# An adaptive FFN kernel: 32-bit copies of q1's transposes, an offset taken off through a tenth row of b1, and new orders of all engines

## The chip, the cores and the metric

The kernel runs on one core of a Trainium2 chip. The metric is the device time of one execution in microseconds (us). Engines: PE is TensorE (matrix multiplies and transposes), ACT is ScalarE, DVE is VectorE, POOL is GpSimd, SP is SyncE, whose queue starts the DMA transfers.

## The reference

The input x is 2 x 1024 tokens of 256 numbers. With a condition vector per batch, weights are made for a small down/up pair; then two quantised layers follow, each with its own scale per token and one per weight matrix:

```python
y   = x + relu(x @ w_down) @ w_up                     # w_down 256x64, w_up 64x256, per batch
h   = rmsnorm_quant(y) @ quant(w1).T + b1             # 256 -> 1024
h   = gelu(h)
out = x + rmsnorm_quant(h) @ quant(w2).T + b2         # 1024 -> 256
# act_quant: s = 127 / max|v| per token, round(v*s)/s;  weight_quant: s = 1/mean|w|, clip(round(w*s), -1, 1)/s
```

## The kernel before

Tokens are taken in 8 pairs of tiles (`PAIRS`), a pair being 128 tokens of each of the two batches; s = 0 or 1 (`SLOTS`) is the batch. For a pair k the steps are these.

- `down(n)` (PE, L250) for a group of one or two pairs, `relu(n)` (ACT), `up(k)` (PE, L274), `add_x(k)` (DVE, L735) give y. `square_y(k)` (ACT) sums its squares, `largest_y(k)` (DVE, L653) takes its largest value, `first_steps` and `first_multipliers` make step and multiplier, `quantise_y(k)` (DVE, L704) writes q1.
- q1 is in words of 32 bits whose low half is, as an f16, 1536 + q: adding `MAGIC` rounds and leaves q there. `transpose_q1(k)` (PE, L282) transposes those halves into PSUM, f16; `copy_q1t(k)` (ACT, L534) copies the 512 columns out and takes the 1536 (`OFFSET`) off.
- `first_layer(j, s)` (PE, L301): four matmuls of 512 columns into `h[s]`. `add_bias(j, s)` (PE, L311): b1, split into three bf16 parts by `split_b1(0)` and `split_b1(1)` (DVE, L740), is multiplied by the inverse scale of each token, itself split into three parts by POOL (`inverse_parts`, L1047), so `PARTS` = 9 rows. The inverse scales go through `transpose_inv` (PE) and `copy_invt` (ACT, L540).
- `gelu(j, s)` (ACT, L508) reads `h[s]`; `square_g` (ACT), `largest_g` (DVE, L647), a step and a multiplier, `quantise_first` (slot 0) or `quantise_second` (slot 1) (DVE, L687) write q2, again 1536 + q. `transpose_q2` (PE, L320), `copy_q2t` (ACT, L545, which copies 512 words of 32 bits and leaves the offset in), `second_layer(j, s)` (PE, L336; its first matmul takes the offset off, with the column sums `w2s` made by `sum_w2`), `combine(j, s)` (DVE, L724), and a store by SP once both slots are combined. The last pair is stored slot by slot, slot 0 first. `combine` and `second_layer` of a pair wait for both slots of it or of the pair before.
- Weights: |w1| and |w2| are summed by ACT and DVE (`abs_sum_w1`, `abs_sum_w2`), `weight_sum` (PE) adds over partitions, `total_weights`, `weight_scale`, `inverse_weight_scale` (DVE) give the scale; `round_...`, `lower_...`, `clip_...` make `w1q` and `w2q` in parts (w1: three, w2: two).
- POOL also makes the dequantising factors (`dequantisers(i)`, L996) and adds b2 to x (`add_b2(j)`, L989). `keep_busy` (PE, L233) is matmuls on zeros while PE has nothing to do.

What sets the order is a list of calls written out for each engine (PE from L358, ACT from L560, DVE from L834, POOL from L1066); each engine works through its own list, and semaphores hold it where an input is missing. No engine skips ahead.

Of the kernel before, what the change touches and what calls it, by code (L numbers as in the profile page):

```python
# [4 lines left out]
P = 128  # L5
SLOTS = 2
PAIRS = 8
D, H, F = 256, 64, 1024
DK, FK = D // P, F // P
HALF = 512  # L10
# [9 lines left out]
def adaln_ffn(nc, x_both, down_pack, up_pack, w1_t, w2_t, b1_rows, b2_rows, out):  # L20
# [3 lines left out]
    with ExitStack() as ctx:  # L24
# [38 lines left out]
        w2s = sb("w2s", [P, D], F16)  # L63

# [43 lines left out]
        q1t_view = q1t_ps.rearrange("p (s k t) -> p s k t", s=SLOTS, k=DK)  # L108
        invt_view = t0_flat[:, HALF:HALF + SLOTS * P].bitcast(BF16).rearrange("p (s t) -> p s t", s=SLOTS)
# [42 lines left out]
        w2s_summed, w2s_ready, b1_rest = sem("w2s_summed"), sem("w2s_ready"), sem("b1_rest")  # L152
        up_done, y_ready, xb_ready = sem("up_done"), sem("y_ready"), sem("xb_ready")
# [19 lines left out]
        B1_ROWS = 32 + PARTS  # L173

        def half_rows(n):
            return slice(32 * n, 32 * n + PARTS)
# [55 lines left out]
        def _(pe):  # L232
# [116 lines left out]

            def sum_w2():  # L350
# [16 lines left out]
            keep_busy(6)  # L367
            weight_sum(0)
            down(1)
            transpose_q1(0)  # L370
            keep_busy(3)
            up(1)
            first_layer(0, 0)
            transpose_inv(0)
            first_layer(0, 1)
            add_bias(0, 0)
            down(2)
            transpose_q1(1)
# [12 lines left out]
            sum_w2()
            up(4)
            transpose_inv(2)
            first_layer(2, 0)
            transpose_q2(0, 1)
            add_bias(2, 0)
            first_layer(2, 1)
            transpose_q2(1, 0)
            add_bias(2, 1)
            second_layer(0, 1)  # L400
            transpose_q1(3)
            up(5)
            second_layer(0, 0)
            transpose_q2(1, 1)
# [3 lines left out]
            add_bias(3, 0)  # L408
            second_layer(1, 0)
            second_layer(1, 1)  # L410
            transpose_q2(2, 0)
            down(4)
            add_bias(3, 1)
            transpose_q2(2, 1)
            up(6)
            transpose_q1(4)
            second_layer(2, 0)
            second_layer(2, 1)
            transpose_inv(4)
            first_layer(4, 0)  # L420
            transpose_q2(3, 0)
            add_bias(4, 0)
            first_layer(4, 1)
            up(7)
            transpose_q1(5)
            add_bias(4, 1)
            transpose_q2(3, 1)
            second_layer(3, 0)
# [3 lines left out]
            add_bias(5, 0)  # L432
            second_layer(3, 1)
            transpose_q2(4, 0)
            add_bias(5, 1)
            transpose_q2(4, 1)
            transpose_q1(6)
            second_layer(4, 0)
            transpose_inv(6)
            first_layer(6, 0)  # L440
            second_layer(4, 1)
            add_bias(6, 0)
            transpose_q2(5, 0)
            first_layer(6, 1)
            transpose_q2(5, 1)
            transpose_q1(7)
            add_bias(6, 1)
            second_layer(5, 1)
            transpose_inv(7)
            first_layer(7, 0)  # L450
            add_bias(7, 0)
            first_layer(7, 1)
            add_bias(7, 1)
            second_layer(5, 0)
            transpose_q2(6, 0)
            transpose_q2(6, 1)
            second_layer(6, 0)
            transpose_q2(7, 0)
            second_layer(6, 1)
            transpose_q2(7, 1)  # L460
            second_layer(7, 0)
            second_layer(7, 1)

        @block.scalar
        def _(a):
            a.wait_ge(b1_zero, 1)
            for n in range(2):
                a.dma_start(b1f[half_rows(n), :], b1_rows[:, HALF * n:HALF * (n + 1)]).then_inc(b1_in, 16)
# [95 lines left out]
            round_w1()  # L564
            relu(1)
            lower_w1()
            abs_sum_w2()
            copy_q1t(0)
            copy_invt(0)
            square_y(1)  # L570
            gelu(0, 0)
            relu(2)
            gelu(0, 1)
            copy_q1t(1)
            square_y(2)
            round_w2()
            copy_invt(1)
            lower_w2()
            gelu(1, 0)
            copy_q2t(0, 0)  # L580
            relu(3)
            square_g(0, 1)
            copy_q1t(2)
            gelu(1, 1)
            square_g(0, 0)
            copy_invt(2)
            square_y(3)
            copy_q2t(0, 1)
            gelu(2, 0)
# [3 lines left out]
            copy_q1t(3)  # L593
            square_g(1, 1)
            copy_invt(3)
            square_g(1, 0)
            copy_q2t(1, 1)
            square_g(2, 1)
            gelu(3, 0)
            square_g(2, 0)  # L600
            copy_q2t(2, 0)
            relu(4)
            square_y(5)
            copy_q2t(2, 1)
            gelu(3, 1)
            copy_q1t(4)
            square_g(3, 1)
            copy_invt(4)
            square_g(3, 0)
            copy_q2t(3, 0)  # L610
            gelu(4, 0)
            square_y(6)
# [544 lines left out]
```

## Time and profile before

| | us |
|---|---|
| median of 3 runs (lowest, highest) | 84.02 (83.64, 84.12) |
| the profiled execution, its own time | 84.57 |
| its span, from first to last instruction | 82.9 |
| TensorE clock granted | 1.00 of full speed |

The rows further down come from that one profiled execution. A duration in a timeline is that of one instruction (xN: of N merged); neighbours on an engine overlap somewhat, so the distance between two starts is shorter than the duration. In brackets stands the time that the engine was idle before, and what ended it. The chain of waits is the work that ended last, followed back from the end. "issue" is time in which an engine waited for nothing that the profile shows.

### The profile page before, as it was taken

Reading aid. Unit: us, or ns where it says so; the run is one execution under the profiler, and the core shown is the slowest. Engines: PE = TensorE matmul, PEld = TensorE weight load, DVE = VectorE, ACT = ScalarE, POOL = GpSimd, SP = SyncE. Lnnn points to the kernel's source line nnn. Section 1 sums busy time; section 2 is a strip of 40 time slices with the busy share of each in tenths; the row PEclk is TensorE's granted clock in tenths of the full one; section 3 lists DMA queues with packets and bytes.
Section 4 is the critical chain, followed back from the end, with each engine's and each line's share of the span. In section 5 each row is a group of like instructions: output and inputs, shape, how many; then the busy total and the mean of one; then the engine's idle time right before and its main releaser. Section 6 shows DMA issues by size and latency. Waiting matters only on the chain.

```text
span 82.9 us, 1692 instructions
## 1 busy us (share of the span) xinstructions
PE 68.6 (83%) x507; PEld 39.9 (48%) x507; DVE 71.6 (86%) x153; ACT 65.3 (79%) x127; POOL 44.1 (53%) x113
## 2 busy tenths in 40 slices
PE   4989717599799449899999999999999999948740
PEld 1533215034354134376666594484765662836730
DVE  2158859999899999999999999989999989999950
ACT  0601198838899997969999999999999999999600
POOL 6800007856459989970078183079604872975140
PEclk9999999999999999999999999999999999999999
DMA  0887999999300000000030200300030030002033
GB/s 26 260 296 265 405 342 425 427 415 382 125 4 4 0 12 0 4 0 0 0 126 9 116 11 0 127 0 8 0 127 0 0 127 0 12 21 106 0 127 127
DMA packets 3212, 9.18 MB, mean 111 GB/s; under 512 B 370, under 2 KB 882, under 8 KB 2820
## 3 DMA queue, kind: packets, MB, share of 16 engines
q1 hardware_dynamic: 3168, 9.05, 28.9%
q8 instruction: 4, 0.07, 0.3%
q14 instruction: 4, 0.03, 0.1%
q10 hardware_dynamic: 36, 0.04, 0.1%
HBM read 6.98 MB, written 2.10 MB: 110 GB/s over the span
## 4 chain that ended last, share of the span: by engine, by line
PE 42%; DVE 23%; DMA 10%; issue 8%; POOL 6%; ACT 4%; SPq 3%; DVEq 1%; POOLq 0%; ACTq 0%
PE out_ps L347 11%; DMA w<-w_t 10%; PE h L309 10%; DVE mx L650 7%; PE q2t_ps L333 6%; PE up_ps L279 5%; PE h L316 4%; DVE q L691 4%; DVE w2q L823 2%; POOL rms L1024 2%; PE out_ps L345 2%; PE q2t_ps L290 2%; DVE step L659 2%; DVE y L738 2%; DVE mx L655 2%
## 5 line engine op out<-in xcount | busy, mean ns | idle before, releaser
L650 DVE TENSOR_REDUCE mx<-g 128x1 f32<-128x1024 f32 x16 | 19.4, 1210 | 0.5 <-ACT g L513 0.3
L513 ACT ACTIVATE g<-h,deq 128x1024 f32<-128x1024 f32 x16 | 18.2, 1137 | 0.2 <-PE h L316 0.2
L521 ACT ACTIVATE junk<-g,sq_scale 128x1024 bf16<-128x1024 f32 x15 | 17.5, 1172 | 0.0
L309 PE MATMUL h<-w1q,q1t 128*128 128x512 f16 x64 | 16.0, 380 | 1.5 <-ACT q1t L537 1.5
L347 PE MATMUL out_ps<-w2q,q2t 128*128 128x256 f16 x112 | 14.4, 273 | 0.0
L691 DVE TENSOR_SCALAR q<-g,m 128x1024 f32<-128x1024 f32 (+1 forms) x16 | 13.1, 825 | 0.1
L1009 POOL TENSOR_TENSOR var<-ms,eps_w 128x2 f32<-128x2 f32 (+1 forms) x10 | 2.8, 278 | 19.4 <-ACT junk_y L531 10.1
L347 PEld LDWEIGHTS out_ps<-w2q,q2t 128*128 128x128 f16 x112 | 10.9, 98 | 1.6 <-issue 0.3
L993 POOL TENSOR_TENSOR xx<-xx,b 128x512 f32<-128x512 f32 x8 | 10.1, 1273 | 1.7 <-DMA b<-b_rows 1.6
L548 ACT ACTIVATE q2t<-q2t_ps 128x512 f32<-128x512 f32 x16 | 9.9, 617 | 1.4 <-PE q2t_ps L333 1.4
L333 PE MATMUL q2t_ps<-ident,q 128*128 128x128 f16 x128 | 9.7, 220 | 1.4 <-DVE q L691 1.4
L1011 POOL TENSOR_TENSOR rms<-var,neg_half 128x2 f32<-128x2 f32 (+1 forms) x10 | 9.9, 994 | 0.8
L333 PEld LDWEIGHTS q2t_ps<-ident,q 128*128 128x128 f16 x128 | 7.8, 98 | 4.7 <-DVE q L691 2.9
L309 PEld LDWEIGHTS h<-w1q,q1t 128*128 128x128 f16 x64 | 5.5, 98 | 7.6 <-ACT q1t L537 2.4
L279 PE MATMUL up_ps<-wu,act 128*128 128x512 f32 x16 | 8.6, 619 | 0.1
L531 ACT ACTIVATE junk_y<-y,sq_scale 128x256 bf16<-128x256 f32 x14 | 7.1, 527 | 0.2 <-DVE y L738 0.2
L236 PE MATMUL q2t_ps<-idle 128*128 128x512 bf16 x17 | 5.6, 453 | 1.2 <-DVE idle L834 1.2
L732 DVE SCALAR_TENSOR_TENSOR xx<-out_ps,deq,xx 128x256 f32<-128x256 f32 x14 | 6.3, 473 | 0.2 <-issue 0.2
L738 DVE TENSOR_TENSOR y<-up_ps,xx 128x512 f32<-128x512 f32 x8 | 5.5, 684 | 1.0 <-PE up_ps L279 1.0
L316 PE MATMUL h<-b1f,invt 9*128 9x512 bf16 x32 | 6.2, 393 | 0.0
L655 DVE TENSOR_REDUCE mx<-y 128x2 f32<-128x512 f32 x8 | 5.4, 676 | 0.0
L478 ACT ACTIVATE junk_w<-w 128x1024 bf16<-128x1024 f32 (+1 forms) x3 | 2.7, 910 | 3.2 <-DMA w<-w_t 3.1
(109 smaller groups left out, 113.2 us busy)
## 6 DMA issues: line engine op xcount, KB each, us to landing
xx<-x_both SPq DMA_DIRECT2D x3, 1024.0 KB, 14.0
w<-w_t SPq DMA_DIRECT2D x4, 512.0 KB, 9.3
out<-xx SPq DMA_DIRECT2D x7, 256.0 KB, 2.0
xx<-x_both SPq DMA_DIRECT2D x2, 256.0 KB, 4.9
xx<-x_both SPq DMA_DIRECT2D x1, 512.0 KB, 9.3
upk<-up_pack SPq DMA_DIRECT2D x1, 384.0 KB, 3.5
out<-xx SPq DMA_DIRECT2D x2, 128.0 KB, 1.8
dpk<-down_pack SPq DMA_DIRECT2D x1, 129.0 KB, 2.1
```

The source lines that it names most:

```text
L279: pe.matmul(up_flat, act[:, k, :], wu[:, :, :].rearrange("p s n -> p (s n)"), start=True, stop=True)\
L309: pe.matmul(h[s][:, cols], q1t[:, j % 2, s, c, :], w1q[:, c, cols], start=(c == 0), stop=False)
L316: mm = pe.matmul(h[s][:, HALF * n:HALF * (n + 1)], invt[half_rows(n), j % 2, s, :], upper_half(b1f[half_rows(n), :]), start=False, stop=True)
L333: mm = pe.transpose(q2t_ps[s][:, c, :], low_half(q2[:, j % 2, s, P * c:P * (c + 1)]), ident[:, :])
L347: mm = pe.matmul(out_bank(j, s), q2t[:, j % 2, s, c, :], w2q[:, c, :], start=False, stop=(c == FK - 1))
L513: a.activation(g[:, j % G_RING, s, :], h[s][:, :], ACT.Gelu, scale=deq[:, col:col + 1])\
L521: a.activation(junk[:, j % 2, s, :], g[:, j % G_RING, s, :], ACT.Square, scale=sq_scale[:, 0:1], accum_out=ms[:, col:col + 1]).then_inc(gs ...
L548: a.activation(q2t[:, j % 2, s].rearrange("p k t -> p (k t)").bitcast(F32), q2t_words[s], ACT.Copy)\
L650: v.tensor_reduce(mx[:, col:col + 1], g[:, j % G_RING, s, :], AX.X, ALU.max, apply_absolute_value=True)\
L691: v.tensor_scalar(q2[:, j % 2, s, cols], g[:, j % G_RING, s, cols], m[:, col:col + 1], MAGIC, ALU.mult, ALU.add).then_inc(ready, 1)
L993: p.tensor_tensor(x[:, j], x[:, j], b2[:, :].unsqueeze(1).broadcast_to([P, SLOTS, D]), ALU.add)\
L1011: p.tensor_tensor(rms[:, cols], var[:, cols], neg_half[:, first:last], ALU.pow).then_inc(rms_done, 1)
```

## The change

q1's transposes are copied out of PSUM as 256 words of 32 bits, two f16 halves each, with no offset taken off. The offset comes off through a tenth row: `inv` gets a column that holds -1536 in each half's block, and the matching row of `b1f` gets the column sums of w1q. Those sums are made once by `sum_w1` on PE (a 32-column weight `pick`, whose column 9 is ones, puts them into partition 9 or 41) and added to `b1f` by `add_w1_sums` on DVE. `add_bias(0, s)` and `down(2)`, which uses the same bank, wait for it.

```diff
+        pick = sb("pick", [P, 32], F16)
...
+        q1t_words = q1t_ps.bitcast(F32)
...
-        B1_ROWS = 32 + PARTS
+
+        B1_ROWS = 32 + PARTS + 1
 
         def half_rows(n):
-            return slice(32 * n, 32 * n + PARTS)
+            return slice(32 * n, 32 * n + PARTS + 1)
 
...
                 else:
                     pe.wait_ge(x_in[n], 16)
+                if n == 2:
+                    pe.wait_ge(w1s_ready, 1)
                 if n == 4:
...
                 pe.wait_ge(invt_ready, j + 1)
                 if j == 0:
-                    pe.wait_ge(b1_rest, 2)
+                    pe.wait_ge(w1s_ready, 1)
                 for n in range(F // HALF):
...
+            def sum_w1():
+
+                pe.wait_ge(pick_set, 1)
+                for n in range(F // HALF):
+                    for c in range(DK):
+                        pe.wait_ge(w1_ready[0 if c == 0 else 1 + n], 1)
+                        mm = pe.matmul(q2t_words[1][32 * n:32 * n + 32, :], pick[:, :], w1q[:, c, HALF * n:HALF * (n + 1)],
+                                       start=(c == 0), stop=(c == DK - 1))
+                mm.then_inc(w1_summed, 1)
+
             def sum_w2():
...
             a.wait_ge(b1_zero, 1)
             for n in range(2):
-                a.dma_start(b1f[half_rows(n), :], b1_rows[:, HALF * n:HALF * (n + 1)]).then_inc(b1_in, 16)
+                a.dma_start(b1f[32 * n:32 * n + PARTS, :], b1_rows[:, HALF * n:HALF * (n + 1)]).then_inc(b1_in, 16)
...
                 wait(a, ffn1_done[1], k - 1)
-                a.activation(q1t[:, k % 2].rearrange("p s k t -> p (s k t)"), q1t_ps, ACT.Copy, bias=-OFFSET)\
+                a.activation(q1t[:, k % 2].rearrange("p s k t -> p (s k t)").bitcast(F32), q1t_words, ACT.Copy)\
                     .then_inc(q1t_ready, 1)
...
 
+            def add_w1_sums():
+                v.wait_ge(w1_summed, 1)
+                v.wait_ge(b1_rest, 2)
+                v.tensor_tensor(b1f[0:B1_ROWS, :], q2t_words[1][0:B1_ROWS, :], b1f[0:B1_ROWS, :], ALU.add)\
+                    .then_inc(w1s_ready, 1)
...
             shift_down()
+            split_b1(0)
             scale_up()
             shift_up()
-            split_b1(0)
+            split_b1(1)
             add_x(0)
             largest_y(0)
             first_steps(-2)
...
             p.memset(inv[:], 0.0)
+            p.memset(pick[:], 0.0).then_inc(zero_set, 1)
             p.memset(neg_offset[:], -OFFSET)
+            p.wait_ge(zero_set, 4)
+            for n in range(2):
+                p.memset(inv[:, :, :, 32 * n + PARTS:32 * n + PARTS + 1], -OFFSET)
+            p.memset(pick[:, PARTS:PARTS + 1], 1.0).then_inc(pick_set, 1)
 
             first_scales()
+            weight_constants(0)
             first_weight_scale()
             inverse_parts(0)
-            weight_constants(0)
+            weight_constants(1)
             dequantisers(-1)
...
```

All four lists are rewritten. They are, in the changed kernel, for PE:

```
keep_busy(5) condition_down() condition_up() keep_busy(1) down(0) keep_busy(2) up(0) keep_busy(8) weight_sum(0)
transpose_q1(0) down(1) keep_busy(2) up(1) keep_busy(4) weight_sum(1) transpose_inv(0) sum_w1() first_layer(0,1)
first_layer(0,0) add_bias(0,1) down(2) add_bias(0,0) down(3) transpose_q1(1) up(2) transpose_inv(1) first_layer(1,0)
up(3) add_bias(1,0) first_layer(1,1) transpose_q2(0,0) add_bias(1,1) up(4) transpose_q1(2) sum_w2() first_layer(2,0)
transpose_inv(2) first_layer(2,1) transpose_q2(0,1) add_bias(2,0) up(5) transpose_q2(1,0) add_bias(2,1)
second_layer(0,0) second_layer(0,1) transpose_q1(3) down(4) transpose_inv(3) first_layer(3,0) first_layer(3,1)
add_bias(3,0) transpose_q2(1,1) transpose_q2(2,0) up(6) add_bias(3,1) transpose_q1(4) second_layer(1,0)
second_layer(1,1) transpose_inv(4) first_layer(4,0) first_layer(4,1) add_bias(4,0) add_bias(4,1) transpose_q2(3,0)
second_layer(2,0) transpose_q2(2,1) transpose_q1(5) up(7) transpose_inv(5) first_layer(5,0) first_layer(5,1)
add_bias(5,0) add_bias(5,1) second_layer(2,1) transpose_q2(4,0) transpose_q2(3,1) second_layer(3,0) transpose_q1(6)
second_layer(3,1) transpose_inv(6) first_layer(6,1) transpose_q2(4,1) add_bias(6,1) first_layer(6,0) transpose_q2(5,0)
add_bias(6,0) second_layer(4,1) transpose_q1(7) second_layer(4,0) transpose_inv(7) first_layer(7,1) add_bias(7,1)
first_layer(7,0) transpose_q2(5,1) add_bias(7,0) second_layer(5,0) transpose_q2(6,1) second_layer(5,1)
transpose_q2(6,0) transpose_q2(7,1) second_layer(6,1) second_layer(6,0) transpose_q2(7,0) second_layer(7,1)
second_layer(7,0)
```

ACT:

```
relu(0) abs_sum_w1(0) abs_sum_w1(1) square_y(0) round_w1() lower_w1() relu(1) copy_q1t(0) abs_sum_w2() square_y(1)
copy_invt(0) round_w2() gelu(0,1) relu(2) gelu(0,0) relu(3) copy_q1t(1) lower_w2() copy_invt(1) square_g(0,1)
square_y(2) gelu(1,0) copy_q2t(0,0) gelu(1,1) copy_q1t(2) square_g(0,0) square_y(3) copy_invt(2) square_g(1,0)
gelu(2,0) copy_q2t(0,1) copy_q2t(1,0) gelu(2,1) square_y(4) copy_q1t(3) square_g(2,0) relu(4) copy_invt(3)
square_g(1,1) gelu(3,0) copy_q2t(2,0) copy_q2t(1,1) square_y(5) copy_q1t(4) gelu(3,1) square_g(2,1) copy_invt(4)
square_g(3,1) gelu(4,0) copy_q2t(3,0) gelu(4,1) copy_q1t(5) square_g(3,0) copy_q2t(2,1) copy_invt(5) square_y(6)
gelu(5,0) gelu(5,1) copy_q2t(4,0) copy_q2t(3,1) square_g(4,0) copy_q1t(6) square_y(7) copy_invt(6) square_g(4,1)
copy_q2t(4,1) gelu(6,1) copy_q2t(5,0) gelu(6,0) copy_q1t(7) square_g(5,0) copy_invt(7) square_g(5,1) gelu(7,1)
copy_q2t(5,1) gelu(7,0) square_g(6,0) copy_q2t(6,1) quantise_last() copy_q2t(6,0) square_g(6,1) copy_q2t(7,1)
square_g(7,0) copy_q2t(7,0)
```

DVE, after six memsets:

```
set_cond() scale_down() shift_down() split_b1(0) scale_up() shift_up() split_b1(1) add_x(0) largest_y(0)
first_steps(-2) first_multipliers(-2) abs_sum_w1() quantise_y(0) total_weights(0) weight_scale(0)
inverse_weight_scale(0) round_w1(0) lower_w1(0) round_w1(2) clip_w1(0) abs_sum_w2() lower_w1(2) clip_w1(1) clip_w1(2)
total_weights(1) add_x(1) weight_scale(1) largest_y(1) inverse_weight_scale(1) add_w1_sums() first_steps(-1)
round_w2() first_multipliers(-1) lower_w2() quantise_y(1) clip_w2(0) largest_g(0,1) largest_g(0,0) add_x(2)
second_step(0) largest_y(2) first_steps(0) first_multipliers(0) quantise_first(0) add_x(3) clip_w2(1) quantise_y(2)
second_multiplier(0) largest_y(3) quantise_second(0) largest_g(1,0) add_x(4) first_steps(1) first_multipliers(1)
largest_y(4) quantise_first(1) copy_w2_sums() largest_g(1,1) add_x(5) quantise_y(3) largest_g(2,0) combine(0,0)
combine(0,1) first_steps(2) second_step(1) largest_y(5) second_multiplier(1) first_multipliers(2) quantise_second(1)
quantise_first(2) largest_g(2,1) quantise_y(4) largest_g(3,0) first_steps(3) first_multipliers(3) second_step(2)
quantise_y(5) second_multiplier(2) add_x(6) combine(1,1) combine(1,0) quantise_first(3) quantise_second(2)
largest_y(6) largest_g(3,1) largest_g(4,0) largest_g(4,1) first_steps(4) second_step(3) first_multipliers(4) add_x(7)
quantise_first(4) second_step(4) second_multiplier(3) quantise_y(6) quantise_second(3) second_multiplier(4)
combine(2,1) combine(2,0) largest_y(7) quantise_second(4) largest_g(5,0) largest_g(5,1) first_steps(5) combine(3,1)
first_multipliers(5) second_step(5) quantise_first(5) second_multiplier(5) combine(3,0) quantise_second(5)
quantise_y(7) largest_g(6,1) largest_g(6,0) combine(4,0) second_step(6) combine(4,1) second_multiplier(6)
first_steps(6) first_multipliers(6) quantise_second(6) quantise_first(6) largest_g(7,1) second_step(7) largest_g(7,0)
second_multiplier(7) combine(5,0) quantise_last() combine(5,1) first_steps(7) scale_last() first_multipliers(7)
quantise_first(7) square_last() combine(6,0) combine(6,1) combine(7,1) combine(7,0)
```

POOL, after its memsets:

```
first_scales() weight_constants(0) first_weight_scale() inverse_parts(0) weight_constants(1) dequantisers(-1)
inverse_scale(1) inverse_parts(1) add_b2(0) dequantisers(0) inverse_scale(2) inverse_parts(2) add_b2(1)
dequantisers(1) add_b2(2) inverse_scale(3) inverse_parts(3) dequantisers(2) inverse_scale(4) inverse_parts(4)
add_b2(3) dequantisers(3) inverse_scale(5) inverse_parts(5) add_b2(4) dequantisers(4) inverse_scale(6)
inverse_parts(6) add_b2(5) dequantisers(5) inverse_scale(7) inverse_parts(7) dequantisers(6) add_b2(6) add_b2(7)
dequantisers(7) dequantisers(8)
```

## Rows read from the trace of the kernel before

**Rows 1.** The page, part 1: busy time by engine.

```profile
PE 68.6 (83%) x507; PEld 39.9 (48%) x507; DVE 71.6 (86%) x153; ACT 65.3 (79%) x127; POOL 44.1 (53%) x113
```

**Rows 2.** Busy time in stretches of core 0; columns: stretch, its length, then each engine.

```profile
12.00:16.00 4.00, 2.85 (x19) 1.51 (x19) 3.85 (x12) 3.63 (x11) 2.77 (x7) 1.00 1.03 418
...
28.00:32.00 4.00, 2.24 (x14) 1.24 (x14) 4.00 (x8) 3.81 (x7) 3.63 (x8) 1.00 0.02 6
...
36.00:44.00 8.00, 8.00 (x65) 5.42 (x65) 7.78 (x17) 7.95 (x16) 3.11 (x10) 1.00 0.10 35
```

**Rows 3.** The chain of waits in order of time: start us, us, what.

```profile
23.71 1.74 issue
...
27.85 1.62 DVE w2q L823
...
35.40 0.62 PE q2t_ps L333 x8
...
40.12 1.73 PE h L309 x8
```

**Rows 4.** Timeline of DVE: start us, us, engine, line, operation [idle before].

```profile
16.61 0.76 DVE L745 SCALAR_TENSOR_TENSOR b1f<-b1f,later 41x512 f32<-41x512 bf16 x1
...
23.68 1.85 DVE L691 TENSOR_SCALAR q<-g,m 128x1024 f32<-128x1024 f32 x1
...
26.64 1.21 DVE L650 TENSOR_REDUCE mx<-g 128x1 f32<-128x1024 f32 x1
27.77 1.69 DVE L823 TENSOR_SCALAR w2q<-w 128x1024 f16<-128x1024 f32 x1
...
30.84 0.74 DVE L691 TENSOR_SCALAR q<-g,m 128x1024 f32<-128x1024 f32 x1
31.50 0.68 DVE L655 TENSOR_REDUCE mx<-y 128x2 f32<-128x512 f32 x1
32.10 1.21 DVE L650 TENSOR_REDUCE mx<-g 128x1 f32<-128x1024 f32 x1
```

**Rows 5.** Timeline of POOL.

```profile
17.42 0.26 POOL L985 TENSOR_SCALAR eps_w<-iws 128x2 f32<-128x2 f32 x1
...
23.71 1.28 POOL L993 TENSOR_TENSOR xx<-xx,b 128x512 f32<-128x512 f32 x1 [1.62 <-DMA b<-b_rows]
...
27.65 1.27 POOL L993 TENSOR_TENSOR xx<-xx,b 128x512 f32<-128x512 f32 x1
```

**Rows 6.** Timeline of ACT.

```profile
17.83 0.38 ACT L543 ACTIVATE invt<-q2t_ps 128x256 bf16<-128x256 bf16 x1 [1.53 <-PE q2t_ps L298]
...
19.10 1.10 ACT L513 ACTIVATE g<-h,deq 128x1024 f32<-128x1024 f32 x1
...
53.96 0.64 ACT L537 ACTIVATE q1t<-q2t_ps 128x512 f16<-128x512 f16 x1
54.44 1.17 ACT L513 ACTIVATE g<-h,deq 128x1024 f32<-128x1024 f32 x1
55.43 0.66 ACT L548 ACTIVATE q2t<-q2t_ps 128x512 f32<-128x512 f32 x1
55.91 0.46 ACT L543 ACTIVATE invt<-q2t_ps 128x256 bf16<-128x256 bf16 x1
56.17 1.23 ACT L521 ACTIVATE junk<-g,sq_scale 128x1024 bf16<-128x1024 f32 x1
...
57.31 1.22 ACT L521 ACTIVATE junk<-g,sq_scale 128x1024 bf16<-128x1024 f32 x1
...
69.48 2.20 ACT L513 ACTIVATE g<-h,deq 128x1024 f32<-128x1024 f32 x2
```

**Rows 7.** Timeline of PE, the second `down`.

```profile
12.92 0.66 PE L263 MATMUL h<-xx,wd 128*64 128x128 f32 x8 [0.42 <-DMA xx<-x_both]
```

**Rows 8.** Timelines of DVE and of SP's queue, the end.

```profile
79.72 0.88 DVE L732 SCALAR_TENSOR_TENSOR xx<-h,deq,xx 128x256 f32<-128x256 f32 x2 [0.71 <-POOL deq L1016]
...
80.23 0.81 SPq L225 DMA_DIRECT2D out<-xx  x2
```

More of the change, by code:

```diff
@@ L408, in _ @@
             add_bias(3, 0)
+            transpose_q2(1, 1)
+            transpose_q2(2, 0)
+            up(6)
+            add_bias(3, 1)
+            transpose_q1(4)
             second_layer(1, 0)
             second_layer(1, 1)
[L411 to L418, printed above, removed]
             transpose_inv(4)
             first_layer(4, 0)
+            first_layer(4, 1)
+            add_bias(4, 0)
+            add_bias(4, 1)
             transpose_q2(3, 0)
-            add_bias(4, 0)
-            first_layer(4, 1)
+            second_layer(2, 0)
+            transpose_q2(2, 1)
+            transpose_q1(5)
             up(7)
[L425 to L428, printed above, removed]
             transpose_inv(5)
@@ L564, in _ @@
             round_w1()
+            lower_w1()
             relu(1)
-            lower_w1()
+            copy_q1t(0)
             abs_sum_w2()
-            copy_q1t(0)
+            square_y(1)
             copy_invt(0)
-            square_y(1)
+            round_w2()
+            gelu(0, 1)
+            relu(2)
             gelu(0, 0)
-            relu(2)
-            gelu(0, 1)
+            relu(3)
             copy_q1t(1)
+            lower_w2()
+            copy_invt(1)
+            square_g(0, 1)
             square_y(2)
-            round_w2()
-            copy_invt(1)
-            lower_w2()
             gelu(1, 0)
             copy_q2t(0, 0)
-            relu(3)
-            square_g(0, 1)
+            gelu(1, 1)
             copy_q1t(2)
-            gelu(1, 1)
             square_g(0, 0)
+            square_y(3)
             copy_invt(2)
-            square_y(3)
+            square_g(1, 0)
+            gelu(2, 0)
             copy_q2t(0, 1)
-            gelu(2, 0)
             copy_q2t(1, 0)
@@ L858, in _ @@
             round_w1(2)
+            clip_w1(0)
+            abs_sum_w2()
+            lower_w1(2)
             clip_w1(1)
-            lower_w1(2)
-            clip_w1(0)
             clip_w1(2)
+            total_weights(1)
             add_x(1)
-            split_b1(1)
+            weight_scale(1)
             largest_y(1)
+            inverse_weight_scale(1)
+            add_w1_sums()
             first_steps(-1)
+            round_w2()
             first_multipliers(-1)
+            lower_w2()
@@ L868, in _ @@
             quantise_y(1)
-            abs_sum_w2()
+            clip_w2(0)
+            largest_g(0, 1)
             largest_g(0, 0)
             add_x(2)
-            total_weights(1)
+            second_step(0)
             largest_y(2)
             first_steps(0)
-            weight_scale(1)
             first_multipliers(0)
-            inverse_weight_scale(1)
             quantise_first(0)
+            add_x(3)
+            clip_w2(1)
             quantise_y(2)
-            round_w2()
-            largest_g(0, 1)
@@ L882, in _ @@
-            lower_w2()
-            second_step(0)
-            clip_w2(0)
-            clip_w2(1)
             second_multiplier(0)
-            add_x(3)
+            largest_y(3)
             quantise_second(0)
-            largest_y(3)
             largest_g(1, 0)
+            add_x(4)
             first_steps(1)
+            first_multipliers(1)
+            largest_y(4)
+            quantise_first(1)
             copy_w2_sums()
-            first_multipliers(1)
-            quantise_first(1)
@@ L895, in _ @@
-            add_x(4)
+            largest_g(1, 1)
+            add_x(5)
             quantise_y(3)
-            largest_g(1, 1)
+            largest_g(2, 0)
+            combine(0, 0)
+            combine(0, 1)
+            first_steps(2)
             second_step(1)
+            largest_y(5)
             second_multiplier(1)
-            largest_y(4)
+            first_multipliers(2)
             quantise_second(1)
-            largest_g(2, 0)
-            first_steps(2)
-            combine(0, 0)
@@ L905, in _ @@
-            first_multipliers(2)
-            combine(0, 1)
+            quantise_first(2)
             largest_g(2, 1)
-            quantise_first(2)
-            second_step(2)
-            add_x(5)
-            second_multiplier(2)
             quantise_y(4)
-            quantise_second(2)
-            combine(1, 0)
-            combine(1, 1)
-            largest_y(5)
             largest_g(3, 0)
@@ L1106, in _ @@
             inverse_parts(4)
+            add_b2(3)
             dequantisers(3)
@@ L1116, in _ @@
             inverse_parts(7)
-            add_b2(5)
             dequantisers(6)
```

217 lines of the change are left out of this document (113 added, 104 removed).

## The prediction

> **What bounds the kernel now.** The first view is the page's table of busy time [rows 1]: VectorE (DVE) 71.6 us, TensorE (PE) 68.6, ScalarE (ACT) 65.3 of a span of 82.9. Three engines so close say that no engine alone is "the" bound, so the second view is busy time by stretch [rows 2]. From 36 to 44 us PE is busy 8.00 of 8.00, ACT 7.95, DVE 7.78: all full. From 28 to 32 us DVE is full (4.00) and PE is busy only 2.24. So the head is DVE's, the middle is everybody's. The chain of waits [rows 3] agrees: it runs on DVE up to 35.40, then on PE. What the reader should see in its head are two pieces: an "issue" of 1.74 at 23.71 and a 1.62 us `w2q` at 27.85.
>
> The timelines of DVE and POOL explain them [rows 4, 5]. The same form of `quantise` takes 0.74 us at 30.84 but 1.85 at 23.68, just as POOL's b2 addition of 1.28 starts at 23.71. The lowering of w2, L823, takes 1.69 at 27.77, beside the next b2 addition (27.65, 1.27 long). If both are worth the 0.74 of the undisturbed one, 1.85 - 0.74 = 1.1 and 1.69 - 0.74 = 0.95 were lost: **2.05 us of DVE stall in the stage that DVE sets**, both on the chain. The reduction at 26.64 (1.21 long, 1.13 to the next start) shows no such stretch, nor does the one at 32.10 beside POOL's later additions. The Trainium skill says why: GPSIMD Engine Reference, Specifications, has the two engines share SBUF interfaces, with contention for DVE operations in a two-port mode or with two SBUF inputs. The trace agrees by the 1.85 against 0.74.
>
> **The change, part by part.** I work with slots, the distance from one start to the next, since neighbours overlap. On ACT [rows 6]: q1t copy 54.44 - 53.96 = 0.48, gelu 0.99, q2t copy 0.48, invt copy 0.26, square 57.31 - 56.17 = 1.14. On DVE [rows 4]: quantise 0.66 (31.50 - 30.84), `largest_y` 0.60, `largest_g` 1.13. On PE [rows 3]: eight first-layer matmuls 1.73, so 0.87 for one `first_layer`.
>
> *Copy as words.* 512 f16 become 256 words. The invt copy also moves 256 elements out of PSUM and has a slot of 0.26 [rows 6]; the q2t copy shows that 512 words cost 0.48, as 512 halves do, so price goes by elements. I take 0.27: 8 x 0.21 = **1.7 us off ACT**, 0.6 of it in the head. Bounds: nothing (if it stayed at 0.48) and 1.8.
>
> *`sum_w1`.* Four 512-column matmuls before `first_layer(0, 1)`: 4 x 0.216 = 0.87 on PE, once. Its nearest row is that of the same form with 128-column weights; I keep from nothing to the whole 1.73 of eight as the bounds. The Trainium skill, TensorEngine Tiling, Key Properties, lets different tiles run in parallel; here only the second and third matmul are neighbours on different tiles, and by that the sum would be 0.65.
>
> *`add_w1_sums`, `split_b1(1)`.* The addition on DVE reads PSUM once and is 512 columns: like an `add_x` or `largest_y`, 0.60. `split_b1(1)`, 0.76 at 16.61 [rows 4], with slot 0.68, moves to before `add_x(0)`, where DVE waits for `up(0)` and later for w1. DVE's sum stays even. `split_b1(0)` ahead of `scale_up` makes `up(0)` some 0.3 later; that is hidden while DVE and ACT wait for w1's DMA, and costs its 0.3 if w1 came sooner.
>
> *w2's weights earlier.* DVE's `abs_sum_w2` (a 1024-column reduction: 1.13) comes at about 15.3, before the last parts of w1, in place of after `quantise_y(1)`. Is w2 there? x of pair 1 landed at 12.92 [rows 7]; at 418 GB/s [rows 2] the 1.0 MB of w2 behind it needs 2.5 us more: 15.4. Just in time. But it pushes `clip_w1` and `add_x(1)` back by 1.2 us: `add_x(1)` began 0.6 before the split at 16.61, at 16.0, and now begins at 17.3.
>
> *POOL.* `weight_constants(0)` now stands before the first inverse parts: two operations, the first 0.26 with 0.33 to the next start [rows 5], some 0.5 together (the memsets of `pick` and of the new `inv` columns fall into POOL's wait for the first squares and cost nothing; if that wait were gone, they would cost some 0.3), so `transpose_inv(0)` slips from 17.5 (its copy began at 17.83 [rows 6]) to 17.9. Behind it on PE wait `sum_w1` (to 18.9) and both first layers (to 20.6). `add_w1_sums` gets its sums at 19.0 and is done at 19.6; the bias follows the layers, at 20.95. So **the first gelu starts at 21.05 instead of 19.10** [rows 6]: 1.95 us late. That hurts less than it sounds: ACT fills the wait with `square_y(1)` and with `round_w2`, which used to come behind both gelus, and part of the 1.53 that it waited before the first invt copy [rows 6] goes.
>
> *b2 additions.* `add_b2(0)` still waits for its DMA, to 23.7, but DVE then runs `largest_g(0, 0)` and `add_x(2)`, which don't stall; `round_w2` and `lower_w2` have run by 21.3, and `add_b2(1)` comes only at 30.8. By the new order the 2.05 us of stall are gone, but for up to 0.65 at `first_steps(1)`.
>
> **The sum, by walking the new order with these slots** (each operation starts when its engine is free and its inputs are done; 0.1 us per hand-over). At some places I compare with the time at which the kernel before had done the same set of operations:
> - DVE starts `largest_g(1, 0)` at 29.65; before 32.10 [rows 4]. 2.4 ahead, 2.05 of it from the stall; `add_w1_sums` (0.6) is made up by the moved split (0.68).
> - PE starts the first layers of pair 3 at 38.16; before 40.12 [rows 3]. It has done `down(4)` by then (eight matmuls, 1.0), which it had not, and lacks one `transpose_q2` (0.45): 2.0 + 1.0 - 0.45 = 2.5 ahead.
> - From there on PE is the tight engine. Counted in the same way at pairs 5 and 6, its lead grows by 0.3 only, because nothing on PE became cheaper.
> - The last gelu ends at 68.2; before 69.48 + 2.20, so 71.6 [rows 6]: 3.4 ahead. Slot 1 of the last pairs goes first, so that `largest_g(7, 1)` and ACT's last copies no longer stand in one line behind the last gelu.
> - The last combine ends at 76.1 by the walk. For the work of DVE after 36.6 the walk sets 2.2 us less than the trace before holds for the same set (small steps and stalls); half of it or less fits into gaps that the walk has. So 77.0; before 80.60 [rows 8]. 3.6 ahead.
> - The stores of slots 0 and 1: SP waits for slot 0 first, and slot 0 is now combined last, so both issues (0.81 together [rows 8]) come behind the last combine, where before one did: **0.4 worse**.
>
> 3.6 - 0.4 = 3.2 us off the span. The profiled execution took 84.57 (span 82.9, 1.67 around it), 0.55 over the median of 84.02. 82.9 - 3.2 = 79.7 of span, 81.4 for that execution, and 84.02 - 3.2 = **80.8 us** for the median. About 0.5% (0.4 us) is what a measurement can tell from no change.
>
> **Rivals.**
> - *Only the head's lead stays.* The last pairs give nothing, since DVE has its line of work behind the last gelu (80.60 - 71.68 = 8.9 us before) either way. 2.4 - 0.4 = 2.0: 82.0. For it: DVE was full to the end. Against: slot 1 first takes a reduction out of the last line. Chance 0.20.
> - *The stalls come back elsewhere.* All eight b2 additions (1.27 each) are still made. If a quantise or step starts at the start of two of them, 2.05 is lost again, and ACT's 1.7 less 0.4 remains: -1.3, 82.7. By the rule of the GPSIMD Engine Reference cited above nothing is avoided for good, only placed; by it a shift of half a microsecond decides. Chance 0.15, half of what a blind placement would deserve, since long reductions stand at most places.
> - *Copy by words costs as before* (0.48): 3.2 - 1.7 = 1.5 off, 82.5. The invt row speaks against it. Chance 0.03.
> - *Slower: the late start is never made up.* Place: POOL's inverse parts, `sum_w1` and `add_w1_sums` in line before the first gelu, on an ACT that has little idle time afterwards. +1.95 + 0.4 - 1.7 = +0.65: 84.7. It decides if ACT has no work to fill the wait, that is if the first gelu starts past 21.5 or w2 lands past 16.5, with all of DVE's list (in order) behind `abs_sum_w2`. Against: DVE's own sum is what set the head. Chance 0.10.
> - *A lead lost half-way* through new waits in a rewritten order of three full engines, to within 0.4 us of before: 0.07.
>
> The forecast (79.7 to 81.6; its low end is the walk without DVE's 0.9) keeps 0.45.
>
> **How the numbers follow.** Faster by over 0.5% are the forecast, the first three rivals: 0.45 + 0.20 + 0.15 + 0.03 = 0.83. Same 0.07, slower 0.10. Low end 79.5, a little under the walk's own 79.9. The high end takes in the rivals at 82.0, 82.5 and 82.7 with `sum_w1` at its dear end (+0.9): 83.5. What lies outside is the slower case and most of the even one.
>
> **What the profile would show.** q1t copies of about 0.39 us each; first gelu at 21 on slot 1; no quantise or `w2q` over 1 us before 30 us; PE full from about 33; last gelu ending near 68 to 69; both stores issued behind the last combine, near 77. Wrong if DVE stands waiting for gelus between 22 and 36, if `abs_sum_w2` waits for its DMA, or if the last gelu ends past 70.5.

## The result, and the profile after

The changed kernel takes 81.14 us (median of 4 runs, 81.11 to 81.39); the kernel before took 84.07 in the same series. The ratio is 0.965, with a 95% interval of 0.958 to 0.972. In a later series it was 81.36 against 83.56, ratio 0.972 (0.966 to 0.978). The forecast was 80.8 in a range from 79.5 to 83.5. Medians and ranges from here on leave out the slow runs, those over 1.5% above the fastest of their kernel.

| | before | after |
|---|---|---|
| the profiled execution, its own time, us | 84.57 | 81.12 |
| its span | 82.9 | 79.4 |
| first w1 sum on DVE starts | 11.31 | 10.65 |
| first gelu starts | 19.10 | 20.27 |
| last gelu ends | 71.68 | 68.00 |
| last two combines start | 79.72 | 75.84 |

The lines behind this table that stand nowhere else, first of the kernel before, then of the changed kernel (w1 sum, last gelu, last combines):

```profile
11.31 0.69 DVE L795 TENSOR_REDUCE asum<-w 128x1 f32<-128x512 f32 x1 [0.94 <-DMA w<-w_t]
```

```profile
10.65 0.69 DVE L819 TENSOR_REDUCE asum<-w 128x1 f32<-128x512 f32 x1 [0.15 <-DMA w<-w_t]
...
66.87 1.13 ACT L531 ACTIVATE g<-h,deq 128x1024 f32<-128x1024 f32 x1
...
75.84 0.88 DVE L750 SCALAR_TENSOR_TENSOR xx<-h,deq,xx 128x256 f32<-128x256 f32 x2 [0.32 <-issue]
```

One difference isn't the kernel's. The weights landed 0.66 us earlier in the profile after. The start of the first w1 sum moves by over two microseconds between the profiles of this study (10.65 to 13.00), so from here on I compare profiles by the distance **from the start of the first gelu to the start of the last pair of combines**: 60.62 before, 55.57 after (and 55.56 in a second profile of the same kernel). The kernel before has one profile only, and that execution took 84.57 us, where its medians are 83.42 to 84.07; so a difference to its profile may be too large. The first gelu itself comes 7.79 us behind the first w1 sum before and 9.62 after. Together 68.41 against 65.19: 3.2 us of kernel, of which the store order gives 0.4 back (below).

The page of the changed kernel, parts 1 and 2, answers to [rows 1]:

```profile
PE 69.2 (87%) x515; PEld 40.8 (51%) x516; DVE 69.6 (88%) x154; ACT 63.6 (80%) x127; POOL 44.9 (57%) x117
...
PE   3997937759999999999999999996999999949910
```

DVE is busy 2.0 us less, though it got an addition; ACT 1.7 less; PE 0.6 more. Busy time by stretch answers to [rows 2]:

```profile
20.00:24.00 4.00, 4.00 (x30) 1.86 (x29) 3.57 (x7) 3.73 (x6) 3.47 (x10) 1.00 0.18 69
...
28.00:32.00 4.00, 4.00 (x29) 2.40 (x29) 3.96 (x9) 4.00 (x11) 3.02 (x10) 1.00 0.01 2
...
52.00:60.00 8.00, 7.36 (x71) 5.21 (x71) 8.00 (x19) 8.00 (x20) 5.07 (x11) 1.00 0.10 35
```

PE, which had 2.24 of 4 between 28 and 32 us, is now full from 20 us on (to 52); the prediction had expected it full from about 33. DVE's timeline answers to [rows 4]:

```profile
18.11 0.68 DVE L769 TENSOR_TENSOR b1f<-q2t_ps,b1f 42x512 f32<-42x512 f32 x1
...
19.56 0.70 DVE L847 TENSOR_SCALAR w2q<-w 128x1024 f16<-128x1024 f32 x1
...
25.79 0.75 DVE L709 TENSOR_SCALAR q<-g,m 128x1024 f32<-128x1024 f32 x1
...
29.24 1.21 DVE L668 TENSOR_REDUCE mx<-g 128x1 f32<-128x1024 f32 x1
...
30.96 0.51 DVE L677 SCALAR_TENSOR_TENSOR step<-mx,over_q 128x3 f32<-128x3 f32 x1
...
43.19 1.67 DVE L727 TENSOR_SCALAR q<-y,m 128x256 f32<-128x256 f32 x2
...
67.80 0.82 DVE L677 SCALAR_TENSOR_TENSOR step<-mx,over_q 128x1 f32<-128x1 f32 x1
```

The two long operations of the head are gone: w2q 0.70 for 1.69, quantise 0.75 for 1.85. But two others are long that weren't: the pair of `quantise_y(5)` at 43.19 (1.67, where its like takes 0.61) and a step at 67.80 (0.82, where its like takes 0.15). POOL's timeline has a b2 addition at each, and one at the smaller stretch at 30.96 (0.51):

```profile
30.17 1.28 POOL L1018 TENSOR_TENSOR xx<-xx,b 128x512 f32<-128x512 f32 x1
...
43.38 1.33 POOL L1018 TENSOR_TENSOR xx<-xx,b 128x512 f32<-128x512 f32 x1
...
67.33 2.51 POOL L1018 TENSOR_TENSOR xx<-xx,b 128x512 f32<-128x512 f32 x2
```

ACT's copies and the first gelu, to be read beside [rows 6]:

```profile
22.95 0.38 ACT L555 ACTIVATE q1t<-q2t_ps 128x256 f32<-128x256 f32 x1
23.24 1.14 ACT L524 ACTIVATE w2q<-w,neg_round 128x1024 f16<-128x1024 f32 x1
...
20.27 1.11 ACT L531 ACTIVATE g<-h,deq 128x1024 f32<-128x1024 f32 x1 [0.51 <-PE h L322]
```

### The profile page after: what moved, and what is told of

The parts are those of the page before. It is cut to its first block, busy times and chain, and to the rows that moved or that the text cites. A ratio compares the mean times of both kernels' runs of the same rounds, so it can differ in the third digit from the quotient of the medians.

```text
span 79.4 us, 1717 instructions
## 1 busy us (share of the span) xinstructions
PE 69.2 (87%) x515; PEld 40.8 (51%) x516; DVE 69.6 (88%) x154; ACT 63.6 (80%) x127; POOL 44.9 (57%) x117
## 4 chain that ended last, share of the span: by engine, by line
PE 42%; DVE 18%; issue 10%; DMA 9%; POOL 9%; ACT 3%; SPq 3%; DVEq 2%; POOLq 0%; ACTq 0%
PE h L315 11%; DMA w<-w_t 9%; PE out_ps L353 9%; DVE mx L668 6%; PE up_ps L285 5%; PE h L322 4%; PE q2t_ps L339 4%; DVE q L709 4%; DVE q L727 3%; DVE xx L750 3%; POOL rms L1036 3%; POOL rms L1049 2%; PE out_ps L351 2%; DVE mx L673 1%; PE out_ps L269 1%
## 5 line engine op out<-in xcount | busy, mean ns | idle before, releaser
L1036 POOL TENSOR_TENSOR rms<-var,neg_half 128x2 f32<-128x2 f32 (+1 forms) x10 | 11.5, 1146 | 0.8
L709 DVE TENSOR_SCALAR q<-g,m 128x1024 f32<-128x1024 f32 (+1 forms) x16 | 11.4, 730 | 0.1
L566 ACT ACTIVATE q2t<-q2t_ps 128x512 f32<-128x512 f32 x16 | 9.4, 604 | 0.0
L240 PE MATMUL q2t_ps<-idle 128*128 128x512 bf16 x21 | 6.6, 440 | 1.3 <-DVE idle L858 1.2
L727 DVE TENSOR_SCALAR q<-y,m 128x256 f32<-128x256 f32 x16 | 6.1, 425 | 0.0
L322 PE MATMUL h<-b1f,invt 10*128 10x512 bf16 x32 | 6.0, 392 | 0.0
```

What stands on the lines that cost most here:

```text
L322: mm = pe.matmul(h[s][:, HALF * n:HALF * (n + 1)], invt[half_rows(n), j % 2, s, :], upper_half(b1f[half_rows(n), :]), start=False, stop=True)
L566: a.activation(q2t[:, j % 2, s].rearrange("p k t -> p (k t)").bitcast(F32), q2t_words[s], ACT.Copy)\
L709: v.tensor_scalar(q2[:, j % 2, s, cols], g[:, j % G_RING, s, cols], m[:, col:col + 1], MAGIC, ALU.mult, ALU.add).then_inc(ready, 1)
L1036: p.tensor_tensor(rms[:, cols], var[:, cols], neg_half[:, first:last], ALU.pow).then_inc(rms_done, 1)
```

## The experiments

"The distance" below is that from first gelu to last combines. Where a profile's start was late (last section), its span isn't used.

**The cheaper copy.** In the changed kernel:

```diff
-  a.activation(q1t[...].bitcast(F32), q1t_words, ACT.Copy)
+  a.activation(q1t[...], q1t_ps, ACT.Copy)
```

> The changed kernel with q1t copied as 512 halves (no offset taken off, so the result stays), as dear as before. Theory (ACT's list is one of the tight ones, its 8 x 0.21 us count): +1.7 us if ACT sets the pace throughout, 82.8; between +0.8 and +1.7 is on its side. Rival (PE and DVE set the pace, ACT's saving falls into its own waits): at most +0.3, 81.4.

Measured: 82.31 us (82.21 to 82.36), ratio to the kernel before 0.987 (0.984 to 0.990), where the changed kernel has 0.965 and 0.972. The copies are 0.59 to 0.77 us long, for 0.37 to 0.43; the distance is 56.55, 0.98 more than after. ACT's and DVE's timelines of this kernel:

```profile
23.14 0.60 ACT L555 ACTIVATE q1t<-q2t_ps 128x512 f16<-128x512 f16 x1
```

```profile
43.70 0.61 DVE L727 TENSOR_SCALAR q<-y,m 128x256 f32<-128x256 f32 x2
```

So of 8 x 0.21 = 1.7 us about 1.0 shows. That is the low side of what the theory allowed, and clearly more than the rival's 0.3. It is a net value: with its operations some 0.3 us later, this kernel has `quantise_y(5)` at 43.70 undisturbed (0.61 for 1.67), a stall of 1.06 less, and only 0.4 more of stall elsewhere. The dear copies by themselves may thus cost more than 1.0; how much isn't shown.

**The two halves of the orders.** The old and the new list of each engine have points where both have done the same set of calls. Cut there, and one order is put ahead and the other behind.

```diff
 # newhead_oldrest: new lists up to the cut, old lists behind it; oldhead_newrest: the reverse
 # cut: PE behind 28 calls, ACT 28, DVE 50, POOL 13 (keep_busy, sum_w1, add_w1_sums not counted)
```

> The changed kernel, its four lists cut where both orders have done the same set of calls (PE behind 28 calls, ACT 28, DVE 50, POOL 13): new order ahead of the cut, old order behind it. Theory (the head's lead of 2.4 us, mostly DVE stalls that are gone, is the larger part): 84.07 - 2.4 = 81.7, a little less if the cheaper copies still count behind the cut. Rival (the rest's order made the gain): 83.4 or more.

> The same cut the other way: old order ahead of it (with sum_w1 and add_w1_sums put in), new order behind. Theory: the stalls of 2.05 us in DVE's head stay, only the copies and the last pairs help, 83.0 to 83.5. Rival (the rest's order made the gain): 81.5.

And both old, so that only the copies and the sums are new:

> Old orders on all engines, with the copies as words, sum_w1 behind first_layer(0, 1) and add_w1_sums behind quantise_y(1). Theory (stalls of the head stay; the copies give some of their 1.7 us, sum_w1 and add_w1_sums take 0.6 to 1.2 of it in the head): 83.3 to 84.1. Rival (the copy alone is the change, orders are neutral): 81.5.

The rows come from three series, in which the kernel before took 83.42 (old, old), 83.53 (the two mixed ones) and 83.56 (new, new); the ratios compare best. In the last column the first number moves with the start of the execution as well: among all profiles with the new head it is 8.99 to 10.71.

| orders (all with word copies) | time, us | ratio to before, interval | w1 sum to first gelu + distance |
|---|---|---|---|
| old, old | 84.25 | 1.009 (1.005 to 1.014) | 9.16 + 59.13 = 68.29 |
| old head, new rest | 83.80 | 1.005 (1.001 to 1.010) | 9.16 + 58.23 = 67.39 |
| new head, old rest | 82.86 | 0.992 (0.989 to 0.996) | 9.62 + 57.45 = 67.07 |
| new, new | 81.36 | 0.972 (0.966 to 0.978) | 9.62 + 55.57 = 65.19 |

Three things follow. The copies and sums without new orders are no gain. By the runs they lose 0.8 us (84.25 against 83.42); by the profiles they come out even (68.29 against 68.41; the executions profiled took 85.17 and 84.57, both over their medians). The first gelu waits for the sums (9.16 in place of 7.79), and the distance gives back 1.5 (59.13 for 60.62). DVE's timeline says where from:

```profile
25.79 0.78 DVE L707 TENSOR_SCALAR q<-g,m 128x1024 f32<-128x1024 f32 x1
...
28.80 1.44 DVE L845 TENSOR_SCALAR w2q<-w 128x1024 f16<-128x1024 f32 x1
```

With the gelu late, the first quantise misses the b2 addition, which ended at 24.31 (0.78 for 1.85), and w2q meets it later (1.44 for 1.69). That is 1.3 of the 1.5. Behind the head this kernel has 0.6 more of such stalls than before, so with the old orders the cheaper copies themselves gave between 0.2 and 0.8. It also means that the stall of 2.05 which the last two expectations took to stay was 0.75 (0.78 and 1.45 in the kernel with the old head and the new rest).

The head alone brings 68.29 - 67.07 = 1.2 us, not the 2.4 of its lead; the rest alone brings 0.9. Both bring 3.1, one microsecond more than the two apart. By the ratios it is 1.4, 0.3 and 3.1. Against the expectations, on the scale of 84.07: the new head with the old rest comes to 83.4, the rival's number and not the theory's 81.7, though the rival's reason (the rest alone made the gain) is refuted by the third kernel, which comes to 84.5 where 83.0 to 83.5 was expected. Old with old comes to 84.8, outside its 83.3 to 84.1. So neither half carries the gain alone. What in the new order of the rest gives its part wasn't separated, apart from the last pairs and the stores below.

With the old rest behind the new head, the b2 additions collide at once, as DVE's timeline of that kernel shows beside POOL's (POOL first):

```profile
30.20 4.19 POOL L1017 TENSOR_TENSOR xx<-xx,b 128x512 f32<-128x512 f32 x3
```

```profile
30.58 0.91 DVE L676 SCALAR_TENSOR_TENSOR step<-mx,over_q 128x3 f32<-128x3 f32 x1
31.94 1.31 DVE L708 TENSOR_SCALAR q<-g,m 128x1024 f32<-128x1024 f32 x1
33.77 1.02 DVE L726 TENSOR_SCALAR q<-y,m 128x256 f32<-128x256 f32 x2
```

Undisturbed these three take 0.15, 0.74 and 0.61, so 1.7 us of stall stand within four microseconds of the cut; the changed kernel has 0.6 at the same three (0.51, 0.74 and 0.83).

**Is the stall POOL's, and is it on the path?** In the kernel before:

```diff
 # before_b2_late
-            add_b2(0) ... add_b2(1) ... add_b2(2)  add_b2(3)   (each at its old place)
             inverse_parts(3)
+            add_b2(0)
+            add_b2(1)
+            add_b2(2)
+            add_b2(3)
```

> The kernel before, with the first four b2 additions of POOL moved behind inverse_parts(3), nothing else changed. Theory (the two additions at 23.7 and 27.6 stall quantise and w2q by 2.05 us on the path): the two DVE operations fall from 1.85 and 1.69 to about 0.75, and the time by 1 to 2 us, to 82.0 to 83.0, less what the additions collide with in their new place. Rival (the long operations are slow for another reason, or the stall is not on the path): both stay long, or they get short and the time stays at 84.0.

```profile
23.80 0.78 DVE L691 TENSOR_SCALAR q<-g,m 128x1024 f32<-128x1024 f32 x1
...
26.82 0.68 DVE L823 TENSOR_SCALAR w2q<-w 128x1024 f16<-128x1024 f32 x1
...
37.93 0.62 DVE L659 SCALAR_TENSOR_TENSOR step<-mx,over_q 128x3 f32<-128x3 f32 x1
...
41.46 1.23 DVE L659 SCALAR_TENSOR_TENSOR step<-mx,over_q 128x1 f32<-128x1 f32 x1
```

The cause of the two long operations is shown: quantise falls from 1.85 to 0.78 and w2q from 1.69 to 0.68 when nothing but POOL's list is changed, and the additions, now from 37.26 to 42.67, stretch the steps there. The distance falls by 1.42 (60.62 to 59.20). The time falls less: 83.16 against 83.42, ratio 0.997 (0.993 to 1.001), which doesn't stand out from no change, where 1 to 2 us were expected. By the time alone, the rival's second form (they get short and the time stays) isn't excluded. I leave open why. The times of the kernel before spread from 83.06 to 84.24 us in one series, and its profile is one of 84.57. An addition that begins when b2's transfer lands, 0.03 us behind the start of a quantise, may well hit it in some executions and miss it in others; that wasn't tried.

Then both kernels without the additions:

> The kernel before without the eight additions of b2 (left out: + b2 in the output). Theory (they stall DVE by 2.05 us in the head and by about 1 us later, all in a full DVE list): 84.07 - 2.5 = 81.5, within 0.7. Rival (stalls are absorbed): 83.6 or more.

> The changed kernel without the eight additions of b2 (left out: + b2 in the output). Theory (the new place of the additions already avoids most stalls): 81.14 less 0.3 to 1.0, so 80.1 to 80.8, clearly less than what the kernel before gains. Rival (the stalls came back elsewhere): as much as before, 2 us or more.

The kernel before gains 1.36 us (82.06 against 83.42, ratio 0.981, 0.974 to 0.988), which the rival (83.6 or more) doesn't allow; its distance falls by 2.06. DVE now waits for gelus:

```profile
L650 DVE TENSOR_REDUCE mx<-g 128x1 f32<-128x1024 f32 x16 | 19.4, 1213 | 1.9 <-ACT g L513 1.8
```

DVE waited 0.5 us there in the kernel before. So a part of the stall was worth nothing: ACT would not have been ready. The changed kernel gains 0.49 in distance (55.08), in line with the theory's 0.3 to 1.0, while its time (81.58, 81.02 to 82.11, from four runs) can't be told from no change; in its profile the first `add_x` began 2 us later than after, most of it because PE's first matmuls took about twice as long (last section).

**The last pairs.** New order up to the end, old order behind it:

```diff
 # old_tail, DVE (PE and ACT in the same way)
-            largest_g(7, 1)
-            second_step(7)
             largest_g(7, 0)
...
+            largest_g(7, 1)
+            second_step(7)
```

> The changed kernel with the old order behind a common cut near the end (PE behind 92 calls, ACT 76, DVE 121, POOL 35): slot 0 of the last pair is reduced first, though its gelu still comes second. Theory (slot 1 first takes one reduction out of the line behind the last gelu): +0.7 to +1.3 us, with the reduction of slot 1 behind that of slot 0. Rival (DVE is full to the end either way, order is neutral): within 0.3.

```profile
69.44 1.22 DVE L667 TENSOR_REDUCE mx<-g 128x1 f32<-128x1024 f32 x1 [1.49 <-ACT g L530]
...
72.69 1.21 DVE L667 TENSOR_REDUCE mx<-g 128x1 f32<-128x1024 f32 x1
```

From the last gelu's start to the last combines it takes 9.74 us, against 8.97 after: +0.77. The first part of the way is nearly unchanged (46.72 against 46.60). DVE idles 1.49 where it had the other slot's reduction to do. The old order of the last combines gives 0.4 of it back (next experiment). The time is 81.58 us (two runs, 81.55 and 81.60) against 81.36, ratio 0.975 (0.965 to 0.985): +0.2 where +0.7 to +1.3 was expected, and not clear of no change.

This experiment overstates the swap, because it is an order that no kernel had: in the kernel before, slot 0's gelu comes first as well, and DVE doesn't idle at that reduction. From the end of the last gelu to the start of the last combines the two orders as they are take 8.04 before (71.68 to 79.72) and 7.84 after (68.00 to 75.84), and 8.38 in the kernel with the new head and the old rest. So the swap of slots is worth 0.2 to 0.5 us, stalls included, and the stores below take 0.4 back.

**The store order.**

```diff
-            for s in range(SLOTS):
+            for s in (1, 0):
                 sp.wait_ge(out_ready[s], PAIRS)
```

> The changed kernel with SP waiting for slot 1 before slot 0 at the last pair. Theory (two stores behind the last combine cost one issue): one issue of about 0.4 us leaves the end, 80.7 us against 81.14. Rival (the second store's issue and flight are hidden by the first's): 81.1, no difference.

> SP waits for slot 1 before slot 0 at the last pair, in one series with the changed kernel. Theory (one store issue less behind the last combine): 0.4 us below it, and in the profile 3.2 us from the start of the last combine to the end of the span in place of 3.56. Rival: the same as it.

From the start of the last combines to the end of the span: 3.56 and 3.59 in two profiles of the changed kernel, 3.18 and 3.14 in the two with the stores swapped. That is the 0.4. In time: 81.15 against 81.36 in one series (lowest 80.80 against 81.16), ratios 0.970 (0.964 to 0.976) and 0.972; the first series gave 81.12, the rival's number, with the changed kernel not beside it. The sign is right, the medians alone wouldn't show it.

**A better placing of the additions?**

```diff
-            add_b2(3)
             dequantisers(3)
             inverse_scale(5)
             inverse_parts(5)
+            add_b2(3)
             add_b2(4)
...
+            add_b2(6)
             dequantisers(6)
-            add_b2(6)
 # and DVE's second_step(7) behind largest_g(7, 0), SP's stores as in the last experiment
```

> The changed kernel with add_b2(3) behind inverse_parts(5) (beside three long reductions), add_b2(6) ahead of dequantisers(6), second_step(7) behind largest_g(7, 0), and the stores of the last pair in the order of their combines. Theory (stalls of 1.07 us at quantise_y(5) and of 0.7 us at second_step(7) are on the path, and one store issue): 81.1 - 1.0 - 0.4 - 0.4 = 79.3 at best, 80.0 if half of the stall in the middle is absorbed. Rival (only the store counts): 80.7.

A miss: 81.30 us (81.05 to 81.72), ratio 0.972 (0.965 to 0.979), the same as the changed kernel. DVE's timeline:

```profile
45.03 0.64 DVE L727 TENSOR_SCALAR q<-y,m 128x256 f32<-128x256 f32 x2
...
46.72 0.88 DVE L750 SCALAR_TENSOR_TENSOR xx<-out_ps,deq,xx 128x256 f32<-128x256 f32 x2 [0.40 <-PE out_ps L353]
...
52.81 1.32 DVE L677 SCALAR_TENSOR_TENSOR step<-mx,over_q 128x3 f32<-128x3 f32 x2
```

with the additions of that kernel in POOL's timeline:

```profile
51.54 2.50 POOL L1018 TENSOR_TENSOR xx<-xx,b 128x512 f32<-128x512 f32 x2
```

`quantise_y(5)` is healed (0.64 for 1.67), but 0.4 of the 1.0 won is spent at 46.72 waiting for PE's `second_layer`. And the two additions in a row outlast the reductions beside which I had put them: the steps at 52.81 take 1.32 in place of 0.22, so 1.1 is lost again. To the last gelu it takes 0.68 more than after, from there to the last combines 0.19 less, and the stores save 0.4: even, as the runs say. Only the version with the stores swapped may be said to be ahead of the changed kernel, by the 0.4 that its profile shows.

The second run of the changed kernel, made as the measure for that series:

> The changed kernel once more, as the measure for the other runs of this series: 0.965 of the kernel before by every theory.

It gave the 0.972 of the table.

## Why the prediction was right, and where it wasn't

- **The sum**: 3.2 off the span was forecast, 3.5 came, 0.66 of it from weights that landed earlier. By the medians 2.9 (84.07 to 81.14) and 2.2 (83.56 to 81.36). The forecast was thus at the high end, 0.3 to 1.0 too much. (Its own low end stands once as 79.7 and once as 79.9; 80.8 less 0.9 is 79.9.)
- **The walk** held well at its end. With the second profile of the changed kernel, whose first w1 sum starts at 11.22, near the 11.31 of before: first gelu at 20.85 (forecast 21.05), last gelu's end at 68.57 (68.2), last combines' end at 77.29 (77.0), span 80.0 (79.7). The places between fit less well: `largest_g(1, 0)` at 29.82 (29.65), but the first layers of pair 3 at 38.49 (38.16), where before has 39.95 read in the same way. There the lead was 1.5 and not the forecast 2.0, and it then grew to 3.1 at the last gelu, by more than the walk gave it. Part of the close end is luck: the walk let pass 1.7 us of stall that came back, held 0.9 in reserve for small steps and stalls behind 36.6, and took `sum_w1` 0.33 too dear.
- **DVE's stalls**: "2.05 us of DVE stall gone, but for up to 0.65". Right in place and in cause (w2q undisturbed takes 0.70 and not 0.74, so it was 2.1). 0.36 was kept at `first_steps(1)` (0.51 against 0.15). Mis-sized as a gain on the path: all additions taken out of the kernel before are worth 1.4 to 2.1 us, since ACT's gelus come next; the removal of all the additions takes out the stalls behind the head too. The rival "the stalls come back elsewhere" came true in part: 1.06 at `quantise_y(5)` and 0.67 at `second_step(7)`, which the walk let pass because I took POOL's additions there to be beside combines and reductions.
- **ACT's 1.7 us**: the slot is right (23.24 - 22.95 = 0.29; 0.38 long). About 1.0 shows as a net value, 0.2 to 0.8 with the old orders.
- **`sum_w1`**: I took 0.87; the chain of waits after has 0.54.

```profile
17.52 0.54 PE q2t_ps L362 x4
18.07 1.83 PE h L315 x8
```

  The Trainium skill's rule on tiles (TensorEngine Tiling, Key Properties) gives 0.65 as an estimate, as I applied it, nearer than my row; that the tiles overlap isn't shown by this alone.
- **The head as the larger part**: this is the step that failed. The rival "only the head's lead stays" (82.0) and the first of the expectations on the orders (81.7) took the lead of 2.4 as worth 2.0 to 2.4 at the end whatever follows. The lead at 29.65 was there (`largest_g(1, 0)` at 29.24 against 32.10, 2.2 after the earlier weights), but with the old rest behind it only 1.2 stay, and against the kernel before only 0.7 by the runs (82.86 against 83.53). A lead is worth what the orders behind it keep.
- **The slower rival** came true for the old orders: the first gelu is 1.37 late and the kernel is 0.8 us slower than before (1.009). That the late gelu is the reason is its argument and not shown, since the profiles come out even. The new orders decide on which side the kernel falls.
- **The last pairs and the stores**: from the end of the last gelu to the end of the last combines the walk has 8.8; before has 8.9, and the second profile of the changed kernel 8.7. So the swap of slots gave the small gain that the sum needed. The expectation of +0.7 to +1.3 without it was too high: +0.2 in time. The store costs its 0.4 as forecast.

## What to carry to other kernels

When three engines are nearly full, a cheaper instruction may not show until the orders are written for it: here the same copies, with the sums that they need, were a loss of 0.8 us by the runs with the old lists, and about 1.0 of a gain of 2.2 to 2.9 with new ones. When one edit shifts a timeline by half a microsecond, count the stalls again before putting the difference down to the edit. Look in the timeline for operations of one form whose durations differ (0.74 and 1.85), and at what another engine started at that moment; then place the pair apart, and check that it doesn't meet the next neighbour. Compare profiles from a common point behind the start when the start varies.

## What was unexpected of the hardware

- The start of the same head takes different times: first w1 sum at 10.65 and at 11.22 in two profiles of the changed kernel, at 12.18 and 13.00 in two others of this study. The landing of the inputs is the smaller part. PE's first matmuls take about twice as long in some executions, though the granted clock reads 1.00 there; the first two lines are of the changed kernel, the other two of the last experiment's:

```profile
4.58 1.13 PE L252 MATMUL h<-upk,cond 128*128 128x512 f32 x2
...
5.86 0.66 PE L269 MATMUL h<-xx,wd 128*64 128x128 f32 x8
```

```profile
5.22 2.07 PE L252 MATMUL h<-upk,cond 128*128 128x512 f32 x2 [0.62 <-DMA upk<-up_pack]
...
7.66 1.12 PE L269 MATMUL h<-xx,wd 128*64 128x128 f32 x8
```

  The second profile of the changed kernel has 1.99 for the first of them with no wait ahead of it, and the kernel with the dear copies 1.12 behind a wait of 0.54. What decides it isn't shown.
- From the first gelu on, two profiles of one program agree to 0.01 us (55.57, 55.56) in the changed kernel and to 0.09 (55.59, 55.68) in the one with the stores swapped, though there the first gelu starts at 20.33 in one and at 22.68 in the other.
- The stretched DVE operations end with POOL's addition or a fixed bit behind it, wherever they began. Steps of 0.15 end at 31.47, 34.13 (before) and 68.62, the additions at 31.45, 34.11 and (the first of two) 68.60; the operations of 0.74 and 0.70 end 0.54 behind theirs (25.53 for 24.99, 29.46 for 28.92, both before). By these rows the operation waits for the addition and isn't slowed, so its loss depends on where in the addition's 1.27 us it starts. Reductions (1.21) and additions that read PSUM (0.68) beside the same additions are not stretched.
- POOL seems to be stretched as well. The powers at 72.71 take 1.57 us while DVE runs `square_last` (72.49 to 73.7), and 0.70 at 74.78 beside combines that read PSUM. No experiment moved one of the two. The first lies on the chain behind which the last four combines wait, so the 0.87 may be a cost of the new order's end; before, the same powers at 78.66 took 0.69:

```profile
72.71 1.57 POOL L1036 TENSOR_TENSOR rms<-var,neg_half 128x2 f32<-128x2 f32 x1
...
74.78 0.70 POOL L1036 TENSOR_TENSOR rms<-var,neg_half 128x2 f32<-128x2 f32 x1
```
